# Feed-forward attention: the reciprocal sums laid out by ScalarE and eight transposes, in place of sixteen half-width products

## What is computed

```
logits    = q @ k.T / 8, masked
denom_log = logaddexp(logsumexp(logits), attn_sink)
attn      = exp(logits - denom_log)
y         = attn @ v                      # 16 heads of 64 features
x         = x + (y @ proj_w + proj_b)
```

## Time and profile before

| | |
|---|---|
| median of 3 runs | 1332.41 us (1331.86 to 1332.47) |
| the profiled execution, its time | 1331.51 us |
| the profiled execution, its span | 1329.6 us |
| granted TensorE clock, mean | 0.904 of full speed |
| feed-forward attentions | about 30 to 345 us and 775 to 1097 us |
| experts | about 345 to 500 us and 1097 to 1329 us |
| middle attention | about 500 to 775 us |

### The profile page before, as it was taken

How to read it: one execution, slowest core, us unless ns; L and a number is a source line. 1 busy time by engine, 2 the same in 40 slices (tenths; PEclk the granted TensorE clock), 3 DMA queues, 4 the chain that set the end, 5 groups by cost and what they waited for, 6 DMA issues and landing times.

```text
span 1329.6 us, 24766 instructions
## 1 busy us (share of the span) xinstructions
PE 1012.1 (76%) x7773; PEld 733.2 (55%) x7834; DVE 827.7 (62%) x2064; ACT 565.6 (43%) x2156; POOL 649.6 (49%) x860
## 2 busy tenths in 40 slices
PE   2899999999358854888888959999999990888100
PEld 1567666676347743555555536667666660777100
DVE  4788888886324422777777758898888761343121
ACT  0455555556223421555555616555555650444000
POOL 2234565564756225556553232466555545740575
PEclk9899999999769985899999979999999995899655
DMA  6677777766124320000000011233211101442221
GB/s 187 160 177 183 189 193 183 173 165 144 48 80 138 109 70 20 19 17 19 21 17 7 1 40 56 74 103 102 93 57 43 36 17 32 134 125 84 71 67 51
DMA packets 98779, 116.60 MB, mean 88 GB/s; under 512 B 14816, under 2 KB 73952, under 8 KB 98656
## 3 DMA queue, kind: packets, MB, share of 16 engines
q1 hardware_dynamic: 76688, 57.73, 13.8%
q10 hardware_dynamic: 10704, 34.21, 12.3%
q0 software_dynamic: 11264, 23.09, 6.2%
HBM read 38.37 MB, written 55.71 MB: 71 GB/s over the span
## 4 chain that ended last, share of the span: by engine, by line
PE 44%; DVE 10%; POOL 8%; issue 6%; POOLq 2%; ACT 2%; DMA 2%; DVEq 0%; SPq 0%; ACTq 0%
PE ps L911 6%; PE ps L819 6%; PE ps L801 5%; POOL shared L1690 4%; PE ps L930 4%; PE ps L706 4%; PE ps L774 3%; PE ps L836 3%; PE ps L740 2%; PE ps L922 2%; PE ps L847 2%; POOLq L474 2%; PE ps L901 2%; DVE shift L1081 2%; DVE pT L1086 1%
## 5 line engine op out<-in xcount | busy, mean ns | idle before, releaser
L1371 ACT ACTIVATE prob<-ps,shift 128x128 f32<-128x128 f32 (+1 forms) x768 | 312.5, 422 | 137.1 <-DVE shift L1081 136.1
L1081 DVE TENSOR_REDUCE shift<-ps 128x4 f32<-128x512 f32 (+1 forms) x192 | 182.6, 951 | 45.0 <-PE ps L803 19.8
L819 PE MATMUL ps<-tb,prob 128*128 128x128 f32 x1152 | 171.8, 285 | 0.1
L1086 DVE COPY pT<-ps 128x512 f32<-128x512 f32 x192 | 131.7, 686 | 46.3 <-PE ps L819 45.9
L819 PEld LDWEIGHTS ps<-tb,prob 128*128 128x128 f32 x1152 | 123.8, 142 | 64.4 <-issue 58.6
L1371 ACT ACTIVATION_READ_ACCUMULATOR prob<-ps,shift 128x1 f32 x768 | 158.7, 207 | 0.0
L1606 POOL DMA_INDIRECT routed<-row_out,row_at x128 | 130.7, 1021 | 26.3 <-issue 24.7
L1680 POOL DMA_INDIRECT qT<-routed,rows_at x96 | 91.7, 956 | 74.2 <-PE ps L901 29.0
L836 PE MATMUL ps<-pT,v 128*64 128x256 f32 x768 | 111.5, 395 | 17.2 <-issue 11.9
L774 PE MATMUL ps<-keyT,qT 64*128 64x256 f32 (+1 forms) x1024 | 119.7, 352 | 1.4 <-issue 1.4
L1398 ACT ACTIVATE yraw<-ps 128x256 f32<-128x256 f32 x128 | 49.2, 384 | 160.9 <-PE ps L836 160.3
(11 more groups left out here) (159 smaller groups left out, 1848.6 us busy)
## 6 DMA issues: line engine op xcount, KB each, us to landing
routed<-nothing ACTq DMA_DIRECT2D x16, 2048.0 KB, 12.7
swapped<-rot_b SPq DMA_DIRECT2D x160, 128.0 KB, 2.1
answers<-yraw SPq DMA_DIRECT2D x48, 256.0 KB, 2.3
shared<-in_w_up SPq DMA_DIRECT2D x32, 256.0 KB, 3.2
qT<-routed SPq DMA_DIRECT2D x96, 64.0 KB, 1.9
shared<-in_w_down SPq DMA_DIRECT2D x32, 128.0 KB, 3.4
routed<-row_out,row_at POOLq DMA_INDIRECT x128, 2.4
qT<-routed,rows_at POOLq DMA_INDIRECT x96, 2.7
```

The lines of the kernel that those rows point to most:

```text
L819: last = pe.transpose(ps[:, BANK_SIDE + bank, h * P:(h + 1) * P], prob[:, s % 4, h, c * P:(c + 1) * P], ident)
L1081: dve.tensor_reduce(shift[:, lt % 2, 4 * g:4 * g + 4], score_view(L, s, lt), AX.X, ALU.max, negate=True)\
L1086: dve.tensor_copy(pT[:, s % 2, 0, :], ps[:, BANK_SIDE + L.turned[k, s][0][0], :]).then_inc(S["pT_ready"], 1)
L1371: last = act.activation(prob[:, s % 4, h, 0:keys(lt)], score_view(L, s, lt)[:, h, :], ACT.Exp, bias=shift[:, lt % 2, one:one + 1], accum_o ...
```

## The change

The sixteen products per tile, each of one head's reciprocal column (repeated 64 times by a stride of zero) with the identity, give way to eight full-width transposes of a buffer `head_wide` that holds each reciprocal 64 times. ACT fills it with two copies per tile, one for each half of the heads, 512 columns each, between its copy to `yraw` and its exps. DVE's reciprocal writes its 16 results in another order, so that the two heads of a transpose lie side by side. The spread steps now wait for ACT (`wide_ready`) and no longer for DVE; ACT waits for the reciprocals and for the previous tile's products (`yT_ready`). The middle attention is left as it was.

```diff
@@ PE, tail_step, "spread" @@
-                        pe.wait_ge(*S.at("rinv_ready", tile + 1))
                         if L.ffn:
+                            pe.wait_ge(*S.at("wide_ready", 2 * tile + half + 1))
                             for n in range(4):
-                                for side in range(2):
-                                    h = 8 * half + 4 * (n // 2) + 2 * side + n % 2
-                                    last = pe.matmul(misc[DH * side:DH * side + DH, n * P:(n + 1) * P],
-                                                     rinv[:, lt % 2, h:h + 1].broadcast_to([P, DH]), ident,
-                                                     start=True, stop=True)
+                                at = 8 * half + 2 * n
+                                last = pe.transpose(misc[:, n * P:(n + 1) * P],
+                                                    head_wide[:, at:at + 2, :].rearrange("p h d -> p (h d)"), ident)
                         else:
+                            pe.wait_ge(*S.at("rinv_ready", tile + 1))
@@ DVE, normaliser @@
-                        dve.reciprocal(rinv[:, lt % 2, :], denom[:, lt % 2, :]).then_inc(S["rinv_ready"], 1)
+                        dve.reciprocal(rinv[:, lt % 2, :].rearrange("p (g n s) -> p g s n", n=2, s=2),
+                                       denom[:, lt % 2, :].rearrange("p (g s n) -> p g s n", s=2, n=2))\
+                            .then_inc(S["rinv_ready"], 1)
@@ ACT @@
+                def widen(k, lt):
+                    tile = 4 * k + lt
+                    act.wait_ge(*S.at("rinv_ready", tile + 1))
+                    act.wait_ge(*S.at("yT_ready", 2 * tile))
+                    for half in range(2):
+                        heads = slice(8 * half, 8 * half + 8)
+                        act.activation(head_wide[:, heads, :], rinv[:, lt % 2, heads].unsqueeze(2).broadcast_to([P, 8, DH]),
+                                       ACT.Copy).then_inc(S["wide_ready"], 1)
...
+                        if L.ffn:
+                            for kk, lt in at_slot(frame, (6, 10, 14, 18)):
+                                widen(kk, lt)
                         if frame.unit(0):
                             k, s = frame.unit(0)
                             exps(k, s)
```

More of the change, by code:

```diff
@@ L158 @@
     pT_full=(8, 8), pT_ready=(8, 8), pT1_ready=(4, 4), yraw_ready=(8, 2), y_full=(0, 2), sink_diff=(2, 2), sink_shift=(2, 2),
-    sink_exp=(2, 2), denom=(2, 2), inverse=(0, 2), rinv_ready=(2, 2), null_step=(0, 2), yT_ready=(4, 2), vz_zero=(0, 1),
+    sink_exp=(2, 2), denom=(2, 2), inverse=(0, 2), wide_ready=(4, 0), rinv_ready=(2, 2), null_step=(0, 2), yT_ready=(4, 2), vz_zero=(0, 1),
     base_ready=(1, 0), x1_ready=(2, 2), square_ready=(2, 0), rms_step=(4, 0), h2_ready=(2, 0), h2T_ready=(2, 0),
@@ L385, in build @@
         rinv = sb("rinv", [P, 2, H])
+        head_wide = sb("head_wide", [P, H, DH])
         rinv_wide = sb("rinv_wide", [P, 2, H, VD])
```

## The result

The changed kernel takes 1343.88 us (median of 4 runs, 1340.45 to 1346.87) beside 1332.13 us for the kernel before on the same chip: ratio 1.0088, interval 1.0063 to 1.0113. So the change costs 12 to 14 us. The forecast was 1336 us with a range up to 1341; sign right, size wrong.

A forecast was written before the change was run, and what follows sets the result against it. PE looked like the bound, but in wide frames the chain leaves it for DVE and ACT. Terms 3.4 + 2.8 - 2.0 - 1.2 + 0.8 = +3.8 us gave 1336 us, range over the cases 1329 to 1341.

The forecast's parts named there:

- The narrow frames: Ten narrow frames with a rope behind: exps 0.59 us later, rope waits for `h2T`, 0.38 lost per frame, sum +3.4.
- The price of a copy: Each of ACT's two widening copies per tile was taken at 0.49 us, with bounds of 0.42 and 0.56.
- The open wide frames: Four wide frames without enough ACT idle time before exps: one loses 0.95 us, three 0.5 to 0.8, sum +2.8.
- The ends: Ends of each layer: frames 6, 10, 58 gain 0.34 us each, 62 gains 0.6, 66 loses 0.4.
- The covered wide frames: Eight wide frames where ACT's idle time hides the widening and PE's gain is worth nothing, as `place` waits: cost 0.
- The rival that had the chance of 0.02: Clock falls to 1.2 GHz in spread frames, transposes not counting as products: up to 150 us, 1480 us; chance 0.02.
- PE's saving survives: Exps' delay is covered: ten narrow frames gain 0.34 us each, wide frames cost nothing; -5.8, 1326.6 us; chance 0.12.
- ACT hides it all: With copies of about 0.3 us both effects cancel in narrow frames; total 1331 us; chance 0.13.
- DVE and POOL meet differently: Shifted timing against POOL changes `xn` and `hh` times, some 6 us either way: 1330 or 1342 us; chance 0.2.

The follow-up runs named there:

- widening first: The change in narrow frames alone, with ACT's widening copies moved ahead of its copy to `yraw`; 1327.94 us, ratio 0.9972 to the kernel before.
- the same order on the kernel before: The kernel before, with only ACT's copy to `h2T` moved ahead of the frame's exps; 1319.49 us, ratio 0.9907.
- only the narrow frames changed: The change in narrow frames alone, wide frames keeping the kernel before's products; 1331.75 us, ratio 1.0009 to the kernel before.
- transposes as a filling: The changed kernel, with eight discarded transposes on PE before each of the two spread steps of a wide frame; 1337.39 us, ratio 1.0045 to the kernel before.
- less work: The kernel before, with half the products of each wide frame's spread left out and nothing added; 1337.05 us, ratio 1.0060.

## Why the prediction was right or wrong, point by point

**The narrow frames: right.** ACT and PE in a narrow frame of the second layer, timeline of after (start us, us, engine, line, what, idle before):

```profile
874.94 0.39 ACT L1409 ACTIVATE yraw<-ps 128x256 f32<-128x256 f32 x1 [1.12 <-PE ps L836]
875.22 1.14 ACT L1393 ACTIVATE head_wide<-rinv 128x512 f32<-128x512 f32 x2
875.95 0.94 PEld L728 LDWEIGHTS ps<-tb,head_wide 128*128 128x128 f32 x8 [0.61 <-ACT yraw L1409]
876.26 0.36 ACT L1373 ACTIVATE prob<-ps,shift 128x128 f32<-128x128 f32 x1
877.63 0.39 ACT L1424 ACTIVATE h2T<-ps,col 128x128 f32<-128x128 f32 x1
878.07 0.51 PEld L707 LDWEIGHTS ps<-xT,wf 128*128 128x128 f32 x3 [0.87 <-ACT h2T L1424]
```

The exps start 1.32 us behind the start of `yraw`, against 0.67 before: 0.65 later, where 0.59 was worked out. The spread loads in 0.94 and ends 1.18 ahead of the rope, which stands there waiting 0.87 us for `h2T`. The waits of after have it ten times, as many as were named (one frame of the first layer lost next to nothing, as forecast: 0.03):

```profile
PEld ps L707 <- ACT h2T L1424: 8.3, 10, 0.9
```

The frame's loss is 0.37 us by the trace, 0.38 by the sum. The chain of after shows PE's pieces replaced by ACT's:

```profile
875.22 1.14 ACT head_wide L1393 x2
876.36 1.40 ACT prob L1373 x8
877.76 0.27 ACT h2T L1424
...
878.07 1.13 PE ps L707 x4
```

**The price of a copy: right.** 620 ns busy and a pitch near 0.52 (875.22 to 876.26 for two), between the bounds of 0.42 and 0.56. Reading SBUF did not make it cheaper than the copy out of PSUM, 620 against 606 ns; the lower bound rested on that. ACT's busy time rose by 31 us, not by 39: 64 times 0.6 counts the overlap of a copy with the next one twice.

**The open wide frames: right in size.** Frame 54 of the second layer lost 0.65 (0.5 to 0.8), frames 14 and 54 of the first 1.04 and 0.8 (0.95, and 0.5 to 0.8). Frame 46 of the first layer, with a stretch in it, can't be told apart.

**The ends: sign right, some mis-sized.** In the second layer frames 6, 10 and 58 gave -0.84, -0.46 and -0.2 for -0.34 each, frame 62 -0.7 for -0.6, frame 66 about +0.8 (with the rest of the tail; its spread's loads alone end 0.34 later) for +0.4. Together -1.4, against -1.2.

**The covered wide frames: ACT's side right, PE's side wrong; this is the step that failed.** The prediction said that ACT's idle time hides the widening, and it does. Timeline of after, wide frame 22:

```profile
894.31 1.15 ACT L1393 ACTIVATE head_wide<-rinv 128x512 f32<-128x512 f32 x2 [0.43 <-DVE rinv L1104]
895.05 0.42 PEld L728 LDWEIGHTS ps<-tb,head_wide 128*128 128x128 f32 x4 [0.60 <-DVE v L1059]
895.72 0.47 ACT L1373 ACTIVATE prob<-ps,shift 128x256 f32<-128x256 f32 x1 [0.26 <-DVE shift L1081]
896.33 0.42 PEld L728 LDWEIGHTS ps<-tb,head_wide 128*128 128x128 f32 x4 [0.86 <-DVE pT L1086]
898.45 0.10 PEld L750 LDWEIGHTS ps<-picked,mk 128*128 128x128 bf16 x1 [1.70 <-ACT h2T L1424]
899.40 2.08 PE L774 MATMUL ps<-keyT,qT 64*128 64x256 f32 x8
```

The exps still wait for the row maximum (0.26). But then: "PE's gain there is worth nothing either, as `place` waits for `h2T`." Nothing was the wrong price; it is less than nothing. The saved time turned into waiting, as the waits ahead of `place` show, first before, then after (total us, times, longest):

```profile
PEld ps L750 <- ACT h2T L1413: 11.7, 12, 1.3
```

```profile
PEld ps L750 <- ACT h2T L1424: 20.6, 12, 1.7
```

and after the longer wait TensorE runs at 1.2 GHz for a while: the eight records of the scores take 2.08 us, where the same eight took 1.13 in before:

```profile
897.17 1.13 PE L774 MATMUL ps<-keyT,qT 64*128 64x256 f32 x8
```

Windows of a wide frame in before (6 us from `weigh` to `place`, then 3.4 us):

```profile
890.30:896.30 6.00, 4.44 (x49) 3.19 (x49) 5.12 (x8) 3.06 (x11) 2.94 (x4) 1.00 0.08 25
896.30:899.70 3.40, 3.29 (x26) 2.09 (x28) 1.97 (x4) 0.81 (x3) 1.37 (x3) 1.00 0.03 11
```

and of two wide frames of after:

```profile
892.35:898.35 6.00, 3.60 (x25) 2.35 (x25) 5.18 (x8) 4.17 (x13) 3.00 (x4) 1.00 0.08 25
898.35:901.75 3.40, 3.30 (x17) 1.94 (x19) 0.97 (x4) 0.52 (x2) 1.37 (x3) 0.61 0.00 1
973.35:979.35 6.00, 3.61 (x25) 2.35 (x25) 5.18 (x8) 4.17 (x13) 3.00 (x4) 1.00 0.07 22
979.35:982.75 3.40, 3.30 (x27) 2.04 (x28) 1.97 (x4) 0.79 (x3) 1.37 (x3) 1.00 0.00 1
```

PE's busy time ahead of `place` went from 4.44 to 3.60 us, and in the first of these frames the granted clock then falls to 0.61, where it stays at 1.00 in before. By the frames' start times a fall costs 1.6 us and the long one (frame 46 of the first layer) 2.5, so the seven cost about 12 us. The second frame has the same 3.61 us and no fall. So falls appear when work is taken away there and go when it is filled in again, but which frames are hit is settled by no row here, and it changes from execution to execution (seven and nine). One of the seven stands apart: a stretch at 62 to 65 us, in frames 5 and 6 of the first layer, is also in "widening first" and in "the same order on the kernel before", which keep all products of these frames. So the account is shown for the falls from frame 14 on; that early one can have another cause.

With 12 us on top of the forecast's 3.8 the profiled execution would be 16 us above before; it is 9 above. So the falls alone are more than the whole loss, and the forecast had the sign right by luck: its own +3.8 us is not what made the kernel slower. The difference isn't in the second layer, where the terms add up; most of it is in the first, as in "only the narrow frames changed", whose terms make about +2.8 (3.4 - 4 x 0.34 + 0.8) and whose span is 1.4 us shorter than that of before. One piece of it, a stall of 1.6 us, is shown in the last section; the rest stays open.

**The rival that had the chance of 0.02 was the right one, with the wrong mechanism.** The falling clock was argued from the kind of work, transposes for products, and priced as if all frames with a spread ran slowly (150 us). The Trainium skill ("TensorE: Matmul & The Clock Gate", Part 4: PE-mode transpose) does say that transposes don't count as products do; the runs here don't bear it out, since transposes as a filling bring the clock back to 0.98 and 0.97. What lowered the clock, in the falls from frame 14 on, was that PE had less to do. The prediction had half of what it needed: it knew that PE idles there, from the chain, and that the spread fills part of that idle time; no row of before showed what a longer idle time costs. It asked what the saving would gain there, not what the spread's work had been holding up.

**The other rivals.** "PE's saving survives" and "ACT hides it all" are out for the change as it stands: the rope waits for `h2T` ten times. With `h2T` ahead of the exps the change is worth -13.5 us, but not in the way of these rivals: the narrow frames give back 0.09 each and not 0.34, and the wide frames 0.55 to 1.48. "DVE and POOL meet differently" didn't act in the change (`hh` sums to 18.0 us in both), but with `h2T` first on top of it four meetings dissolve, 7.5 us of DVE's time. That POOL's instruction beside those `hh` is the cause I read from the traces alone; no run separated it.

## What to carry to other kernels

Before taking work from an engine that waits in the same place, ask what that work was holding up: on TensorE a longer idle time can cost the clock of the work behind it, 1.6 us each time here, so that the kernel with fewer products and nothing else changed was 7 us slower. An instruction added to an in-order engine delays all that is queued behind it, so look for the short copy at the end of that queue which another engine waits for, and move it forward first: here two lines of order (the kernel before at -0.9% with them, the changed kernel at -2.0%) turned the change from a loss of 12 to 14 us into a gain of 13.5.

## What had not been expected of the hardware

That the granted clock falls inside a dense attention and soon comes back, in some frames and not in others that look alike: 0.61 behind one wide frame and 1.00 behind the next but one, PE having been busy for 3.60 and 3.61 us ahead of them.

PE also loses time with nothing visible to wait for. In the first layer of before there is a stall of 1.61 us in the middle of eight products of the scores (timeline, weight loads, idle before in brackets):

```profile
304.02 0.30 PEld L774 LDWEIGHTS ps<-keyT,qT 64*128 64x128 f32 x4 [1.61 <-issue]
```

In after the same eight load in one run without it:

```profile
308.18 0.52 PEld L774 LDWEIGHTS ps<-keyT,qT 64*128 64x128 f32 x8
```

It is also gone in "less work" and "only the narrow frames", which have little in common, and the frame is 1.6 to 1.7 us shorter in each of the three. Of all kernels here only "the same order on the kernel before" has it too, again of 1.61 us. In both a fetch of 16 KB by an instruction queue ends close to where it begins (in before the fetch ends at 302.42 and the stall begins at 302.41, in the other at 298.78 and 298.59); but the other such fetches in the attentions of before, some forty, pass without a stall of this kind. So what it is stays open.
